# Value products on four column tiles, with sums that GpSimd adds first, in an attention and network kernel on one Trainium2 core

## The chip, the cores and the metric

The kernel runs on one NeuronCore of a Trainium2 chip. Its engines work side by side, each through its own queue: TensorE (products, into the PSUM banks), VectorE, ScalarE, GpSimd, and SyncE, which here only issues DMA transfers. They wait for each other by semaphores. The metric is the device time of one execution in microseconds (us), the median of several runs.

## What is computed

One block of a transformer on x of shape 4 x 1024 x 512, float32. The lines that matter:

```python
h = _layernorm(x) * (1 + ca) + sa
q = (h @ q_w.T + q_b).reshape(b, s, 16, 32)        # 16 heads of 32
k = h @ k_w.T + k_b                                # one key head, one value head for all
v = h @ v_w.T + v_b
scores = einsum('bqhd,bkd->bhqk', q, k) / 32 ** 0.5, causal, softmax over k
x = x + ga * (einsum('bhqk,bkd->bqhd', attn, v) @ o_w.T + o_b)
h = _layernorm(x) * (1 + cb) + sb
u = fwht(h * SU_ug) / 64                           # Walsh-Hadamard transform over 512
y = silu(u @ W_gate.T * sg) * (u @ W_up.T * su)    # 2048 wide
x = x + gb * (fwht(y * SU_dp) / 64) @ W_down.T * (Wscale_dp * 64)
```

## The kernel before

There are 64 heads in the attention stage (`ALL`, 4 batches of 16) and then 128 steps of the network stage (8 blocks of 512 rows by 16 tiles of the 2048). In the attention stage, every head's scores are kept transposed: keys on the 128 partitions, queries along the row. Only the causal part is computed. It is cut into nine units of up to 512 columns (`UNITS`: key tile, first query, width, column). For each unit TensorE computes scores into one of three score banks (L1468), ScalarE takes their exponent into `probs` (L772), and GpSimd clears the triangle above the diagonal of each 128 x 128 diagonal block (L847), 8 a head.

The softmax needs a maximum for each query beforehand. So beside the score of each unit TensorE computes one slot of scores the other way round (`SLOTS`, L1321), for the head that comes two later (`AHEAD`), into one of three side banks that are used in turn. VectorE reduces each slot to maxima (`reduce_slot`, L868 with the causal mask added and the masked scores written to an SBUF tile that nobody reads, L871 without a mask). After slot 8 `negate_maxima` (L880, L881) negates them. TensorE turns them into rows (`max_top`, L1328, in the next head, at `TOP_UNIT` = 1, also into a side bank), ScalarE copies these out (L634), and SyncE moves them into the rows of the queries' stack that add -max to the scores.

All side work uses these three banks in an order written out by hand (`side_work`): queries of four heads (2 x 12 products at the start of each fourth head, split by ScalarE and VectorE), layer norm rows of the next batch (`ROWS`), its keys and values in the head with n = 13 (`KV_STEP`; VectorE stacks the keys in `stack_keys` before the maximum slot of the same unit), output tiles of the last batch (`OUT_TILES`, two a head in heads 5 to 8 of a batch, 13 products each), and folding. Folding applies the second Hadamard transform to the rows of W_down, once: a first half ("across", 16 tiles, L1348) whose result is split into a rounded half by ScalarE and a rest by VectorE and stored to DRAM with both halves, and a second half ("along", 16 tiles, L1353), loaded from there, two fp32r products a tile. Both use rings of two buffers.

Value products (`weigh`, L1491): the weights are 64 columns, 32 of values and 32 of ones (`v_ones`), so that the same product gives the output and the sum of the exponents. The 64 columns go to one of two column tiles of TensorE, partitions 0 to 63 or 64 to 127 of a PSUM bank, and both tiles work side by side. `WEIGHED` gives the order: (tile, unit, key tile, first query, width, column). The products of a head stand in two parts. Part 0 (7 products, 1280 columns a tile) stands behind unit 8 and part 1 (5 products, 1024 columns a tile) behind unit 4 of the next head; these places are `PART_ENDS`. ScalarE empties a bank after each part (`evacuate`, L753). Two partial outputs and two partial sums are gathered by SyncE with four transfers a head (`gather`); VectorE adds and scales them once for four heads.

The engines' queues are in order. In a head, ScalarE's order for a unit is: exponent, what is in `ends`, the emptying of a part, then what is in `units`, where the negated maxima's copy is. VectorE's is: the unit's side work, then `ends`, then `prepare` (gains' floor, output weights and bias in head 7, `PROJECTION_STEP`), group work, and layer norm statistics (`STATS`). The square root of the layer norm's variance runs on ScalarE in head 6 of a batch (`ROOT_STEP`), which loads a table for it and then one for the exponent.

## Time and profile before

| | |
|---|---|
| median of 3 runs | 2063.32 us (2062.88 to 2069.54) |
| profiled execution | 2061.69 us |
| its span, first to last instruction | 2059.9 us |
| granted TensorE clock, mean | 0.988 of 2.4 GHz |
| TensorE busy | 1983.1 us (96%), 9120 matmuls |
| VectorE busy | 1196.9 us (58%) |
| ScalarE busy | 791.3 us (38%) |
| GpSimd busy | 149.3 us (7%) |

The span is cut by stage with the table of busy time by stretch. One head of the attention stage is then followed instruction by instruction on TensorE and VectorE. "Busy" of an engine is the union of its instructions, and TensorE's matmuls overlap, so their starts say more than their lengths. An instruction's start is in us from the span's start. PEclk is the granted TensorE clock, where 1.00 is 2.4 GHz.

### The profile page before, as it was taken

The numbers are of one execution on the slowest core, as the hardware profiler recorded it, in microseconds if no ns is written. First come the engines' busy times: TensorE is split into PE (matmuls) and PEld (weight loads), VectorE is DVE, ScalarE is ACT, GpSimd is POOL, SyncE is SP. The second block draws the span as 40 slices with busy tenths as digits, with TensorE's granted clock in tenths as the row PEclk, the third lists the DMA queues.
The fourth block names the chain that finished last, engine by engine and source line by source line (L and its number), as shares of the span: only waits on it lengthen the run. The fifth ranks groups of instructions, "written<-read, shape, count | busy, mean of one in ns | idle before, by whom it ended". The sixth has DMA issues, their size and how long they took to land.

```text
span 2059.9 us, 26392 instructions
## 1 busy us (share of the span) xinstructions
PE 1983.1 (96%) x9120; PEld 1469.9 (71%) x9120; DVE 1196.9 (58%) x2619; ACT 791.3 (38%) x1334; POOL 149.3 (7%) x522
## 2 busy tenths in 40 slices
PE   6999999999999999888999999999999999999998
PEld 3555666666666556545888888888888888888887
DVE  6678677676767665655555454445554454545434
ACT  3456555555556554455222222222212222222121
POOL 0111121111111111111000000000000000000000
PEclk9999999999999999989999999999999999999999
DMA  7443243333433476743534435334353343443431
GB/s 230 114 109 74 76 128 104 102 89 100 110 106 80 144 227 180 231 166 122 202 133 158 144 128 173 123 123 164 123 173 123 130 167 123 139 148 124 158 127 62
DMA packets 113659, 279.82 MB, mean 136 GB/s; under 512 B 27754, under 2 KB 33130, under 8 KB 113400
## 3 DMA queue, kind: packets, MB, share of 16 engines
q1 hardware_dynamic: 104168, 248.71, 39.0%
q10 hardware_dynamic: 9360, 29.43, 4.1%
q8 instruction: 74, 1.21, 0.2%
q14 instruction: 57, 0.47, 0.1%
HBM read 199.15 MB, written 35.93 MB: 114 GB/s over the span
## 4 chain that ended last, share of the span: by engine, by line
PE 53%; DVE 1%; DMA 1%; ACT 0%; issue 0%; SPq 0%; POOLq 0%; POOL 0%; DVEq 0%; ACTq 0%
PE banks L1266 34%; PE banks L1423 16%; PE banks L1491 1%; PE banks L1365 1%; PE banks L1359 1%; DMA upgate_raw<-in_w_ug 0%; PE banks L1468 0%; PE banks L1321 0%; DMA inverse_sums_dram<-sums 0%; DVE out_sb L1042 0%; DVE out_sb L1033 0%; DMA o_group<-o_raw 0%; PE banks L1334 0%; ACT h_crossed_split L691 0%; ACT probs L772 0%
## 5 line engine op out<-in xcount | busy, mean ns | idle before, releaser
L1266 PE MATMUL banks<-h_t_split,w_ring 128*128 128x512 f32 x3072 | 717.3, 389 | 0.8 <-DVE w_ring L1007 0.8
L1266 PEld LDWEIGHTS banks<-h_t_split,w_ring 128*128 128x128 f32 x3072 | 576.5, 188 | 121.0 <-DVE w_ring L1007 1.2
L708 ACT ACTIVATE silu_gate<-banks,scale_upgate 128x512 f32<-128x512 f32 x128 | 88.3, 690 | 800.6 <-PE banks L1266 800.6
L1423 PE MATMUL banks<-d_ring,y_split 128*128 128x512 f32 x1536 | 370.6, 390 | 0.1
L1015 DVE SCALAR_TENSOR_TENSOR y<-banks,scale_upgate,silu_gate 128x512 f32<-128x512 f32 x128 | 95.9, 749 | 433.4 <-ACT silu_gate L708 433.4
L772 ACT ACTIVATE probs<-banks 128x512 f32<-128x512 f32 x576 | 312.3, 597 | 84.6 <-PE banks L1468 79.3
L1423 PEld LDWEIGHTS banks<-d_ring,y_split 128*128 128x128 f32 x1536 | 287.2, 188 | 59.6 <-DVE y_split L1021 0.5
L1491 PE MATMUL banks<-probs,v_ones 128*64 128x512 f32 (+3 forms) x1536 | 292.4, 518 | 1.4 <-POOL probs L847 1.4
L1321 PE MATMUL banks<-k_stack,q_stacks 96*128 96x512 f32 (+3 forms) x768 | 245.7, 363 | 22.2 <-DVE q_split L889 11.2
L1468 PE MATMUL banks<-q_stacks,k_stack 98*128 98x512 f32 (+3 forms) x768 | 250.3, 368 | 4.9 <-ACT probs L772 4.9
L1491 PEld LDWEIGHTS banks<-probs,v_ones 128*64 128x64 f32 x1536 | 123.1, 142 | 161.7 <-issue 138.1
L847 POOL TENSOR_SCALAR_AFFINE_SELECT probs<-probs 128x128 f32<-128x128 f32 x512 | 147.0, 305 | 806.7 <-ACT probs L772 804.1
L1321 PEld LDWEIGHTS banks<-k_stack,q_stacks 96*128 96x128 f32 x768 | 140.1, 191 | 62.4 <-DVE max_all L868 16.7
L1468 PEld LDWEIGHTS banks<-q_stacks,k_stack 98*128 98x128 f32 x768 | 140.7, 191 | 57.7 <-issue 33.1
L871 DVE TENSOR_REDUCE max_all<-banks 128x1 f32<-128x512 f32 x256 | 165.0, 684 | 4.7 <-PE banks L1321 3.9
L1007 DVE TENSOR_TENSOR w_ring<-upgate_raw,w_ring 128x1024 fp32r<-128x1024 f32 x128 | 156.0, 1219 | 17.9 <-ACT w_ring L700 17.6
L868 DVE CUSTOM_DVE_ANT_0 masked_scores<-banks,mask_row,max_all 128x512 f32<-128x512 f32 (+3 forms) x256 | 132.0, 547 | 58.2 <-PE banks L1321 57.4
L753 ACT ACTIVATE o_raw<-banks 128x512 f32<-128x512 f32 x128 | 76.5, 597 | 206.9 <-PE banks L1491 206.9
L868 DVE CUSTOM_DVE_ANT_0 masked_scores<-banks,mask_row 128x512 f32<-128x512 f32 (+3 forms) x256 | 119.9, 486 | 48.0 <-PE banks L1321 46.7
L700 ACT ACTIVATE w_ring<-upgate_raw 128x1024 fp32r<-128x1024 f32 x128 | 135.1, 1056 | 9.4 <-DMA upgate_raw<-in_w_ug 9.4
L1266 PE MATMUL banks<-h_t_split,qw_group 128*128 128x512 f32 x384 | 92.1, 395 | 5.4 <-DVE h_t_split L898 3.0
L1266 PE MATMUL banks<-ow_split,o_split 128*128 128x512 f32 x384 | 94.4, 394 | 2.2 <-DVE max_all L868 2.1
(122 smaller groups left out, 1249.3 us busy)
## 6 DMA issues: line engine op xcount, KB each, us to landing
upgate_raw<-in_w_ug SPq DMA_DIRECT2D x128, 512.0 KB, 4.2
d_ring<-down_split_dram SPq DMA_DIRECT2D x128, 512.0 KB, 3.3
q_stacks<-q_split SPq DMA_DIRECT2D x192, 128.0 KB, 2.6
o_group<-o_raw SPq DMA_DIRECT2D x128, 128.0 KB, 2.3
x<-in_x SPq DMA_DIRECT2D x32, 256.0 KB, 4.3
o_group<-inverse_sums_dram SPq DMA_DIRECT2D x64, 128.0 KB, 2.7
x_and_residual<-in_x SPq DMA_DIRECT2D x32, 256.0 KB, 4.4
x_dram<-x_and_residual SPq DMA_DIRECT2D x32, 256.0 KB, 2.5
```

The costliest lines, as they stand in the source:

```text
L700: nc.scalar.activation(wr[g % 2][:, 0], ugr[g % UG_RING][:], ACT.Copy).then_inc(ug_cast, 1)
L772: nc.scalar.activation(pr[:, u, :], score_bank[:, at % SLOTS_SCORE, :], ACT.Exp, scale=SCALE).then_inc(exped, 1)
L847: last = nc.gpsimd.affine_select(out=triangle, in_=triangle, compare_op=ALU.is_ge, fill=0.0, base=0, pattern=[[1, P]], channel_multiplier=-1)
L868: last = nc.vector.tensor_tensor_reduce(out=masked_scores[:, i % 2, col:col + w], in0=part, in1=mask[:, HALF - w:HALF], scale=1.0, scalar= ...
L871: last = nc.vector.tensor_reduce(out, part, AX.X, ALU.max)
L1007: nc.vector.tensor_tensor(wr[g % 2][:, 1], ugr[g % UG_RING][:], wr[g % 2][:, 0].bitcast(F32), ALU.subtract).then_inc(ug_ready, 1)
L1015: nc.vector.scalar_tensor_tensor(out=y[:], in0=up_bank[:, s, :], scalar=sug[:, 0, f:f + 1], in1=sg[:, s, :], op0=ALU.mult, op1=ALU.mult).t ...
L1266: ins = nc.tensor.matmul(out, weights(a, k), moving(m, k), start=(k == 0 and a + m == 0), stop=(last and k == kts - 1 and a == 1))
L1321: last = nc.tensor.matmul(side[:, r, col:col + w], qst[0:96, s, qt * P:(qt + 1) * P], kst[0:96, b % 2, k0:k0 + w], start=True, stop=True)
L1423: last = nc.tensor.matmul(acc[:, t, :], ys[s][:, a, t * P:(t + 1) * P], dr[g % D_RING][:, m, :], start=(f == 0 and a + m == 0), stop=(f == ...
L1468: last = nc.tensor.matmul(score_bank[:, at % SLOTS_SCORE, col:col + w], kst[0:98, b % 2, kt * P:(kt + 1) * P], qst[0:98, s, q0:q0 + w], st ...
L1491: last = nc.tensor.matmul(obank[half * 2 * HD:(half + 1) * 2 * HD, c, q0 - c * HALF:q0 - c * HALF + w], vs[:, b % 2, kt, :], pr[:, u, col: ...
```

## The change

- Value products use four column tiles of 32 columns. Tiles 0 and 1 hold values, tiles 2 and 3 ones (in part 1 tile 2 holds values for queries from 256 on in its half, too). Parts are now halves of the queries: part 0 the first 512 (8 products, 640 columns a tile), part 1 the second (17 products, 1280 columns a tile). Each bank is written in one part only.
- The exponents of units 3 to 6 are added by GpSimd into `probs_added` (three additions a head), and ones are multiplied with that sum once. Part 1 waits for it. Unit 2 is needed by both parts and gets a second buffer for every other head.
- The parts stand behind units 2 (part 1 of the head before) and 6 (part 0). The turn of the negated maxima is at unit 2. Statistics, rows, output tiles, keys and folding move to other units and heads.
- Gathering takes six transfers a head; the group sum gets one more addition. The masked scores are written back into their bank.
- Folding's first half is stored in plain float32, without VectorE; the second half is one plain float32 product. Its rings have four buffers.
- The square root runs at the start of head 5 with the exponent's table loaded right behind it. Output weights are split at the start of heads 1 and 5, the bias at the start of head 1. Keys are stacked at the ends of units 2 and 6.

The diff, cut to its core:

```diff
-PART_ENDS, PARTS_OF_HEAD = (4, 8), 2
+PART_ENDS, PARTS_OF_HEAD, SHARED = (2, 6), 2, 2
+ADDED = (3, 4, 5, 6)
 WEIGHED = [
-    [(0, 0, 0, 0, 512, 0), (1, 4, 1, 512, 512, 0), (0, 3, 0, 512, 512, 0), (1, 1, 1, 128, 384, 0), (1, 1, 3, 384, 128, 384),
-     (0, 2, 6, 768, 256, 256), (1, 2, 2, 256, 256, 0)],
-    [(0, 5, 2, 512, 512, 0), (1, 6, 3, 512, 512, 0), (0, 7, 4, 512, 512, 0), (1, 8, 5, 640, 384, 0), (1, 8, 7, 896, 128, 384)],
+    [(0, "v", 0, 0, 0, 512, 0), (2, "s", 0, 0, 0, 512, 0), (1, "v", 1, 1, 0, 384, 128), (3, "s", 1, 1, 0, 384, 128),
+     (1, "v", 2, 2, 0, 256, 256), (3, "s", 2, 2, 0, 256, 256), (0, "v", 1, 3, 384, 128, 384), (2, "s", 1, 3, 384, 128, 384)],
+    [(0, "v", 3, 0, 0, 512, 0), (1, "v", 5, 2, 0, 512, 0), (2, "v", 7, 4, 256, 256, 256), (3, "s", 7, 4, 0, 256, 0),
+     (2, "s", 7, 4, 256, 256, 0), (3, "s", 2, 6, 256, 256, 256), (0, "v", 4, 1, 0, 512, 0), (1, "v", 6, 3, 0, 512, 0),
+     (2, "v", 8, 5, 128, 256, 256), (3, "s", 8, 5, 0, 128, 128), (3, "s", 8, 7, 384, 128, 384), (3, "s", None, None, 0, 512, 0),
+     (2, "s", 8, 5, 128, 256, 0), (0, "v", 7, 4, 0, 256, 0), (1, "v", 8, 5, 0, 128, 128), (2, "v", 2, 6, 256, 256, 256),
+     (1, "v", 8, 7, 384, 128, 384)],
 ]
-ROOT_STEP = 6
-OUT_TILES = {5: {2: 0, 6: 1}, 6: {2: 2, 6: 3}, 7: {2: 4, 6: 5}, 8: {2: 6, 6: 7}}
-ROWS = {(9, 4): (0, 0), (9, 8): (0, 1), (10, 4): (0, 2), (10, 8): (0, 3), (11, 2): (1, 0), (11, 4): (1, 1), (11, 8): (1, 2), (12, 4): (1, 3)}
+ROOT_STEP = 5
+OUT_TILES = {5: {4: 0, 8: 1}, 6: {4: 2, 8: 3}, 7: {4: 4, 8: 5}, 8: {4: 6, 8: 7}}
+ROWS = {(9, 2): (0, 0), (9, 6): (0, 1), (10, 2): (0, 2), (10, 6): (0, 3), (11, 2): (1, 0), (11, 4): (1, 1), (11, 6): (1, 2), (12, 2): (1, 3)}
-TOP_UNIT, FIRST_WEIGHED = 1, 6
+TOP_UNIT = 2
+STACK_UNITS = (2, 6)
-PROJECTION_STEP = 7
+PROJECTION_STEPS = (1, 5)
-            units[2].insert(0, ("kv", b + 1, 0))
-            units[5].insert(0, ("kv", b + 1, 1))
+            units[0].insert(0, ("kv", b + 1, 0))
+            units[4].insert(0, ("kv", b + 1, 1))
...
             def step(H):
                 begin, units, ends = side_work(H, ALL)
+                if n == ROOT_STEP and b + 1 < B:
+                    layer_norm_deviations(nc, act, T, eps, b + 1)
+                    nc.scalar.activation(scratch[:], eps[:], ACT.Exp)
...
+            def add_unit(H, i):
+                pool.wait_ge(exped, H * NU + ADDED[i] + 1)
+                if i == 1:
+                    pool.wait_ge(pv_done, H * PARTS_OF_HEAD)
+                else:
+                    pool.wait_ge(added, H * (len(ADDED) - 1) + i - 1)
+                first = pr[:, ADDED[0], :] if i == 1 else sb[:]
+                nc.gpsimd.tensor_tensor(sb[:], first, pr[:, ADDED[i], :], ALU.add).then_inc(added, 1)
+
             for H in range(ALL):
+                for u in range(NU):
+                    if u in TRIANGLES:
+                        clear_triangles(H, u)
+                    if u in ADDED[1:]:
+                        add_unit(H, ADDED.index(u))
...
-                        last = nc.vector.tensor_tensor_reduce(out=masked_scores[:, i % 2, col:col + w], in0=part, in1=mask[:, HALF - w:HALF],
+                        last = nc.vector.tensor_tensor_reduce(out=part, in0=part, in1=mask[:, HALF - w:HALF],
                                                               scale=1.0, scalar=out if k0 else -BIG, op0=ALU.add, op1=ALU.max, accum_out=out)
...
             def fold_tile(key):
-                    for a in range(2):
-                        last = nc.tensor.matmul(side[:, r, :], had[:], again[:, i % 2, a, :], start=a == 0, stop=a == 1)
+                    last = nc.tensor.matmul(side[:, r, :], had[:].bitcast(F32), again[:, i % FOLD_RING, :], start=True, stop=True)
...
             def weigh(H, part):
                 if part == 0:
-                    pe.wait_ge(masked, H * len(TRIANGLES) + 3)
-                    pe.wait_ge(exped, H * NU + PART_ENDS[0] + 1)
+                    pe.wait_ge(masked, H * len(TRIANGLES) + len([u for u in TRIANGLES if u <= SHARED]))
                 else:
                     pe.wait_ge(masked, (H + 1) * len(TRIANGLES))
+                    pe.wait_ge(added, (H + 1) * (len(ADDED) - 1))
+                products = WEIGHED[part]
+                for i, (tile, what, u, kt, col, w, to) in enumerate(products):
+                    weights = vs[:, b % 2, kt, :] if what == "v" else ones32[:]
+                    moving = sb[:, col:col + w] if u is None else pr[:, held(H, u), col:col + w]
+                    last = nc.tensor.matmul(obank[tile * HD:(tile + 1) * HD, part, to:to + w], weights, moving,
```

## Rows read from the trace of the kernel before

**Rows 1.** Busy time of TensorE over the span, from the page.
```profile
PE 1983.1 (96%) x9120; PEld 1469.9 (71%) x9120; DVE 1196.9 (58%) x2619; ACT 791.3 (38%) x1334; POOL 149.3 (7%) x522
```

**Rows 2.** Stretches with busy time (instructions) by engine, PEclk, DMA share, GB/s.
```profile
57.70:958.80 901.10, 848.17 (x4094) 545.01 (x4092) 622.21 (x1775) 493.41 (x941) 146.98 (x512) 0.97 0.44 123
958.80:2059.90 1101.10, 1094.38 (x4882) 906.38 (x4880) 539.39 (x764) 279.69 (x366) 0.00 (x0) 1.00 0.42 142
```

**Rows 3.** Timeline of TensorE, head 35: start, length, instruction, idle before.
```profile
518.51 0.50 PE L1468 MATMUL banks<-q_stacks,k_stack 98*128 98x512 f32 x1
518.85 0.40 PE L1321 MATMUL banks<-k_stack,q_stacks 96*128 96x512 f32 x1
...
520.04 0.50 PE L1321 MATMUL banks<-k_stack,q_stacks 96*128 96x512 f32 x1
...
521.42 1.94 PE L1491 MATMUL banks<-probs,v_ones 128*64 128x512 f32 x10
523.30 0.50 PE L1468 MATMUL banks<-q_stacks,k_stack 98*128 98x512 f32 x1
...
525.52 2.37 PE L1491 MATMUL banks<-probs,v_ones 128*64 128x512 f32 x14
527.83 0.50 PE L1468 MATMUL banks<-q_stacks,k_stack 98*128 98x512 f32 x1
```

**Rows 4.** Timeline of VectorE in the same head.
```profile
519.29 0.69 DVE L868 CUSTOM_DVE_ANT_0 masked_scores<-banks,mask_row 128x512 f32<-128x512 f32 x1 [0.95 <-PE banks L1321]
...
519.90 0.69 DVE L871 TENSOR_REDUCE max_all<-banks 128x1 f32<-128x512 f32 x1
...
525.50 0.55 DVE L868 CUSTOM_DVE_ANT_0 masked_scores<-banks,mask_row 128x384 f32<-128x384 f32 x1
...
527.00 0.08 DVE L868 DVE_READ_ACCUMULATOR2_ANT max_all<- 128x1 f32 x1
...
527.49 0.17 DVE L881 SCALAR_TENSOR_TENSOR neg_max<-max_all,neg_max 128x8 fp32r<-128x8 f32 x1
```

**Rows 5.** The value products as a group, from the page.
```profile
L1491 PE MATMUL banks<-probs,v_ones 128*64 128x512 f32 (+3 forms) x1536 | 292.4, 518 | 1.4 <-POOL probs L847 1.4
```

**Rows 6.** Timeline of VectorE behind an output tile, head 22.
```profile
349.50 0.69 DVE L941 TENSOR_TENSOR x_and_residual<-banks,gain_row 128x512 f32<-128x512 f32 x1 [2.73 <-PE banks L1334]
```

**Rows 7.** Groups of GpSimd by line and form: busy us, mean ns.
```profile
L847 POOL TENSOR_SCALAR_AFFINE_SELECT probs<-probs 128x128 f32<-128x128 f32 x512 | 147.0, 305 | 806.7 <-ACT probs L772 804.1
L833 POOL MEMSET mask_row<- 128x512 f32 x1 | 0.5, 528 | 0.0
```

**Rows 8.** Timeline of SyncE's queue: issues of DMA transfers in head 35.
```profile
525.31 1.22 SPq L414 DMA_DIRECT2D o_group<-o_raw  x2
```

**Rows 9.** Timeline of TensorE, waits in heads 6, 13, 38, 58.
```profile
143.01 0.50 PE L1321 MATMUL banks<-k_stack,q_stacks 96*128 96x512 f32 x1 [1.88 <-ACT neg_max_rows L634]
244.70 0.50 PE L1321 MATMUL banks<-k_stack,q_stacks 96*128 96x256 f32 x2 [1.18 <-DVE max_all L868]
561.57 0.73 PE L1266 MATMUL banks<-ow_split,o_split 128*128 128x512 f32 x2 [1.04 <-DVE max_all L868]
877.05 0.73 PE L1353 MATMUL banks<-fold_again,hadamard 128*128 128x512 f32 x2 [3.08 <-DMA fold_again<-down_across_dram]
```

**Rows 10.** Stretches as in rows 2: heads 8, 13, 58, 62.
```profile
161.80:181.40 19.60, 16.81 (x75) 11.02 (x74) 14.44 (x42) 10.37 (x19) 2.19 (x8) 0.91 0.22 53
230.20:250.10 19.90, 17.64 (x82) 11.49 (x81) 9.73 (x28) 7.29 (x14) 2.19 (x8) 0.91 0.47 129
870.40:891.50 21.10, 16.23 (x57) 8.31 (x55) 11.33 (x33) 8.09 (x15) 2.20 (x8) 0.76 0.92 318
931.70:946.90 15.20, 10.68 (x42) 5.36 (x40) 9.64 (x10) 8.47 (x17) 6.33 (x8) 0.78 0.27 70
```

**Rows 11.** Groups of TensorE: the folding's two products.
```profile
L1348 PE MATMUL banks<-fold_raw,across 128*128 128x512 f32 x32 | 17.4, 626 | 2.5 <-DVE fold_split L959 1.8
L1353 PE MATMUL banks<-fold_again,hadamard 128*128 128x512 f32 x32 | 12.6, 480 | 15.5 <-DVE max_all L868 4.4 <-DMA fold_again<-down_across_dram 3.1 <-ACT neg_max_rows L634 2.9
```

More of the change, by code:

```diff
@@ L360, in side_drained, with held @@
         engine.wait_ge(side_free[r], len([place for place in places.values() if place % SLOTS_SIDE == r]))
+    def held(H, u):
+        return NU if u == SHARED and H % 2 else u
     def free_bank(g, k):
@@ L671, in fold_transfers @@
                             store_fold((kind, i))
-                        if i < 2 and (ALL - left) * NU == H * NU + u + LOAD_BEFORE:
-                            load_fold(kind, i)
+                        if i == 0 and (ALL - left) * NU == H * NU + u + LOAD_BEFORE:
+                            for first in range(FOLD_RING):
+                                load_fold(kind, first)
             def turn(nb, k, bank):
@@ L918, in add_halves @@
                 if half:
+                    chain.link(last)
+                    last = nc.vector.tensor_tensor(on[:, S - REST:S], on[:, S - REST:S], og_rest[:], ALU.add)
                     last.then_inc(group_taken, 1)
```

188 lines of the change are left out of this document (101 added, 87 removed), and 4 rows, old and new, of the table UNITS.

## Prediction

> **What bounds the kernel now.** The page comes first: TensorE is busy 96% of the span, so the question for each edit is what it does to TensorE's order of work [rows 1]. The table by stage shows three stretches: 57.7 us of start, 901.1 us of attention (64 heads), 1101.1 us of network [rows 2]. The change touches the attention stage and its folding; the network's instructions stay as they are. In attention TensorE is busy 848 of 901 us, VectorE 622, ScalarE 493 and GpSimd 147 [rows 2].
>
> The timeline of one plain head (33 or so look like it) runs from score matmul to score matmul, 518.51 to 527.83, 9.32 us [rows 3]. Its value products stand in two lumps: part 1 of the head before from 521.42 to 523.30 (1.88 us) and part 0 from 525.52 to 527.83 (2.31 us), 4.19 us in all. Between lumps a score and a maximum product alternate every 0.235 us or so; the first after a lump takes 0.34 us. Only one of them is held up: the maximum product of unit 2, at 520.04, and by a tenth. It needs the side bank that VectorE's first reduction of the head frees, and that reduction ends at 519.98 [rows 3, 4]. So VectorE already stands right behind TensorE, and the 2.31 us lump is where it catches up: it works on the last two slots from 525.50 to 527.00 and has the negated maxima at 527.66, 0.17 us before the lump ends and three products before they are wanted [rows 3, 4].
>
> **Value products.** A float32 product is two passes (1536 records for 64 x 12 products [rows 5]), each at two cycles a column: part 1 holds 1024 columns for each of two tiles, 1024 x 4 / 2.4 GHz = 1.71 us, and takes 1.88; part 0 holds 1280, 2.13 us, and takes 2.31. So 0.17 to 0.18 us a lump is overhead and the rest columns, on both tiles at once. After the change part 0 has 640 columns a tile on four tiles (1.07 us) and part 1 has 1280 (2.13 us). With the same overhead: 1.24 + 2.30 = 3.54 us, 0.65 less than 4.19, 41 us over 64 heads, if nothing else binds. That four tiles run side by side is in no row; two do. Bounds: all of it (-41 us), or only two at a time, 7680 columns x 4 / 2.4 / 2 = 6.4 us a head instead of 3.2 (+205 us). I take full overlap, since the two tiles keep the full rate each and the order cycles through the tiles.
>
> The Trainium skill (TensorE: Matmul & The Clock Gate, "Measured speedup vs the span model") gives 2.38 times for three column tiles, not 3. By that the four would take 3.2 x 3 / 2.38 = 4.0 us a head, and the change would be worth 53 us less than my sum. No row here shows more than two tiles.
>
> **Where the lumps stand.** Part 1 moves from behind unit 4 to behind unit 2, part 0 from behind unit 8 to behind unit 6, and the product of the negated maxima from unit 1 to unit 2. Now slots 7 and 8 are issued after part 0, and nothing long stands between them and that product. Count from the start of maximum product 7: 0.44 us until VectorE starts (518.85 to 519.29), slots 7 and 8 1.50 (525.50 to 527.00), negation 0.66 (to 527.66) [rows 3, 4]: the negated maxima are there at 2.60. TensorE gets to them after about 2.0 us (eight products of 0.23 to 0.29). Then maximum product 2 needs the bank of slot 0, which VectorE starts only after the negation: + 0.03 + 0.70 + 0.05 = 3.38 us, where TensorE would be at 2.1. So 1.3 us of wait, in two pieces. A second one: ScalarE empties part 1 (0.50 us to its next instruction) before it copies the negated maxima out of their bank (0.25 us), so maximum product 4 starts 0.92 us behind score 3 and not 0.81, and pays 0.1 for weights that aren't preloaded.
>
> The new head from maximum product 7 to the next: 3.38; to part 1, 0.34 + 0.09 = 0.43; part 1 2.30; score 3 to part 0, 0.92 + 0.34 + 3 x 0.24 + 0.32 = 2.30; part 0 1.24; score 7 and on, 0.34. Sum 9.99 us against 9.32: +0.67 us, although the products are 0.65 us shorter.
>
> By kind of head (62 have the product of the negated maxima):
> - 35 plain or nearly so: 35 x 0.67 = +23.5.
> - 15 that begin with queries (5.6 us of products hide the wait): 15 x (0.21 - 0.65) = -6.6.
> - 9 behind an output tile at unit 8. VectorE has to do gain and residual (0.69, and as long again) between slots 7 and 8 [rows 6], and TensorE has only 1.75 us of other products: 4.0 - 1.75 = 2.25 us of wait, 1.6 a head, +14.5.
> - 3 behind transposed values: +0.
> - Some 23 heads have layer norm rows or folding at unit 6 now, and the VectorE and ScalarE work behind it delays slot 7 by 0.4 to 0.5: +10.
> - The last part 1 is 0.43 longer.
>
> Together **+42 us**. VectorE's masked maxima now write to PSUM; no row has such an output. The reduction without a wide output takes as long as the masked one [rows 4], so the output costs nothing now; I take nothing and, for the range, 0.06 us each way on the five in the chain: 47 heads x 0.3 = 14 us.
>
> **GpSimd.** It clears 512 triangles at 0.305 us and is idle otherwise [rows 7]. It now adds three times 512 columns a head. No row has a two-input operation on it; the memset of 512 takes 0.53, and four times a 128-wide select is 1.2. I take 1.2. Part 1 now waits for the sums, and behind that wait stands all of TensorE. From score 3: exponent 4 ends at 1.85, then 3a + 3 x 0.25 + 0.1, and part 1 starts at 9.99 - 2.30 = 7.7: it doesn't bind below a = 1.65 us.
>
> The Trainium skill (GPSIMD Engine Reference, "3.1 Elementwise — side-by-side cycle accounting") gives 4497 ns for an add of 2048 columns, 1.12 us for 512 if it scales; the sum stays the same. No run here shows it yet.
>
> SyncE gathers with six transfers a head and not four, 1.2 us more of issue at 0.6 each [rows 8]: it has 3 + 1 + 6 = 10 in 10 us, 6.3 us, not on the path. VectorE gets one more 256-wide sum in 15 heads, under queries.
>
> **Repairs.** I price each by a head's excess over its kind.
> - Square root: two table loads and the root hold ScalarE in head 6, and TensorE waits 1.88 [rows 9]. Before the queries they are covered. Head 6 takes 13.9 instead of 9.8 us, heads 22 and 38 lose 1.04 each [rows 9]: -6.
> - Output weights and bias: VectorE's work on them pushes the negated maxima of head 8 back; it takes 19.6 us, TensorE busy 16.8, where its kind takes 14.9 [rows 10]: -4.5.
> - Keys: a wait of 1.18 and a clock of 0.91 in head 13, and the same in 29 and 45 [rows 9, 10], 3.6 us each. Keys at units 0 and 4 with the stacking behind the lumps leave some: -8.5.
> - Folding: first half without VectorE and half the bytes, a ring of four. Head 49 -1.8; heads 54 to 57 lose some 2 each and get new waits of the kind above, -3; head 58 takes 21.1 us where 12 would do, with a wait of 3.08 for a load and a clock of 0.76, and head 59 is like it [rows 9, 10]: 16 us of excess, of which the stores and the block's load keep a third, -11; head 62, with the crossing, takes 15.2 us, TensorE busy 10.7 [rows 10], -4. Against that the second half's product in plain float32 is two passes of 0.43, not two of 0.2: the first half's takes 17.4 us for 16 tiles, the second's 12.6 [rows 11], with 0.4 a tile in columns, +6.4. Net -13.4.
>
> Together **-32 us** (-20 to -50).
>
> **Clock.** It falls in heads where TensorE waited 1.5 us or more in a short while (1.18 and 0.34 more; 1.88; 3.08) and stays at 1.00 in those with one wait of up to 1.04 [rows 9, 10]. The new 1.3 us lie between; those behind output tiles lie above. A stretch at 1.2 GHz of the kind seen costs about 1.7 us. I take five new ones less what VectorE catches up meanwhile: +5, between 0 and 60.
>
> **Sum.** The profiled execution took 2061.69 us with a span of 2059.9; +42 - 32 + 5 gives 2076.7. The median of the runs, 2063.32, is 1.6 above the profiled one: **2078 us**.
>
> **Rivals.** A measurement can tell 0.3%, 6 us, from no change.
> - The forecast: 2078, its own range 2060 to 2095, 0.50.
> - A, faster: the wait for the negated maxima is smaller and the repairs give all of their excess. It decides at a wait of some 0.6 us a head. For it: the removed waits are in the rows; against it: the VectorE chain is five rows long and TensorE's part of it three. With half of the wait (-31) and repairs of -45: 2035; with no wait at all (62 x 1.5) 1990. 0.25.
> - B, the clock: half of the 47 waits bring a stretch at 1.2 GHz, 24 x 1.7 = 40 less the 5: 2113. 0.12.
> - C, GpSimd binds: an add over 1.65 us, or VectorE held up by it. At 2.0 us, 3 x 0.35 x 47 = 49: 2127. For it: its only rows are of one input. 0.07.
> - D, the four tiles don't run together: at best +53, 2131, at worst 2283. The change then doesn't do what it says. 0.06.
>
> Most of A and 0.02 of the forecast are faster by over 0.3%; 0.11 of the forecast and 0.02 of A lie within; the rest is slower. Range: 2030 (leaves the better half of A) to 2118 (leaves D and the longer half of C).
>
> **What will show it.** Right: a plain head of 9.9 to 10.1 us; lumps of 2.3 and 1.24 us; TensorE waiting 0.5 to 0.8 us for the negated maxima and again for slot 0's bank; heads 6, 8 and 58 to 62 shorter. Wrong: plain heads of 8.7 us (no wait); part 1 waiting on GpSimd; lumps over 4 us; masked maxima of another length than 0.69; granted clock under 0.95 over attention.

## Result, and the profile after

The changed kernel takes 2190.55 us (median of 4 runs, 2183.77 to 2193.87), the kernel before beside it 2065.49 us (2062.88 to 2069.54): a ratio of 1.060, 95% interval 1.057 to 1.063. The forecast was 2078 us with a range of 2030 to 2118. So the direction was right, and the size was off by more than 100 us, 73 us beyond the end of the range. The profiled execution took 2189.16 us with a span of 2187.4, mean granted clock 0.964 (0.988 before).

The page's busy times of the changed kernel, which answer to [rows 1]:

```profile
PE 2030.1 (93%) x10784; PEld 1510.0 (69%) x10784; DVE 1236.8 (57%) x2621; ACT 791.5 (36%) x1337; POOL 400.0 (18%) x714
```

The stretches of attention and network, which answer to [rows 2] (the stretch, its length, busy time and instructions of TensorE, its weight loads, VectorE, ScalarE, GpSimd, granted clock, DMA share, GB/s):

```profile
60.90:1074.80 1013.90, 881.16 (x5757) 582.60 (x5756) 661.05 (x1775) 493.59 (x944) 398.04 (x704) 0.93 0.38 103
1074.80:2187.40 1112.60, 1105.56 (x4880) 906.73 (x4880) 539.99 (x765) 279.76 (x366) 0.00 (x0) 1.00 0.43 140
```

Of the 127.5 us of longer span 112.8 are in attention (901.1 to 1013.9), 11.5 in the network (1101.1 to 1112.6), where I had taken nothing, and 3.2 in the start, which tells nothing of the change: in the other runs below the start takes 57.9 to 62.1 us, 59.0 and 61.4 in two runs of one kernel. In attention TensorE's idle time goes from 52.9 us (901.1 - 848.2) to 132.7, and its clock from 0.97 to 0.93: 7% of 1013.9 less 3% of 901.1 is 44 us of work that the lower level costs. GpSimd goes from 147 to 398 us.

The waits of TensorE that are new, over the whole span (what waits, for what: us in total, times, longest):

```profile
PE banks L1379 <- DVE max_all L919: 49.9, 77, 1.2
PE banks L1386 <- DVE neg_max L932: 39.0, 41, 4.5
PE banks L1379 <- ACT neg_max_rows L664: 13.0, 27, 0.5
PE banks L1386 <- DVE q_split L940: 12.7, 9, 1.7
```

The first two are the waits of the forecast, for slot 0's bank (L1379 is the maximum products) and for the negated maxima (L1386 is their transpose). The third is for ScalarE's copy of the negated maxima out of their bank, 0.48 us each time where the forecast had a delay of 0.1. The fourth wasn't foreseen: where queries stand ahead of a head, the transpose waits 1.1 to 1.7 us for VectorE's split of the queries, behind which the sums of the head group now stand, too (before, one maximum product waited 0.75 us for that split). A plain head of the changed kernel, as head 35 in [rows 3, 4]. TensorE and then VectorE in head 31, 524.64 to 534.96:

```profile
523.83 0.40 PE L1379 MATMUL banks<-k_stack,q_stacks 96*128 96x384 f32 x2
...
525.63 0.41 PE L1525 MATMUL banks<-q_stacks,k_stack 98*128 98x256 f32 x2
526.59 0.28 PE L1386 MATMUL banks<-ident,neg_max 128*16 128x128 f32 x1 [0.56 <-DVE neg_max L932]
527.49 0.50 PE L1379 MATMUL banks<-k_stack,q_stacks 96*128 96x512 f32 x1 [0.62 <-DVE max_all L919]
527.93 0.62 PE L1547 MATMUL banks<-probs,values 128*32 128x512 f32 x3
...
530.22 0.50 PE L1525 MATMUL banks<-q_stacks,k_stack 98*128 98x512 f32 x1
...
531.21 0.50 PE L1379 MATMUL banks<-k_stack,q_stacks 96*128 96x512 f32 x1
...
532.60 0.62 PE L1547 MATMUL banks<-probs,values 128*32 128x512 f32 x1
...
533.81 0.50 PE L1525 MATMUL banks<-q_stacks,k_stack 98*128 98x512 f32 x1
```

```profile
524.27 0.57 DVE L919 CUSTOM_DVE_ANT_0 banks<-banks,mask_row 128x384 f32<-128x384 f32 x1 [0.39 <-PE banks L1379]
...
525.81 0.14 DVE L919 DVE_READ_ACCUMULATOR2_ANT max_all<- 128x1 f32 x1
...
526.37 0.17 DVE L932 SCALAR_TENSOR_TENSOR neg_max<-max_all,neg_max 128x8 fp32r<-128x8 f32 x1
526.68 0.70 DVE L919 CUSTOM_DVE_ANT_0 banks<-banks,mask_row 128x512 f32<-128x512 f32 x1
```

Part 1 lasts from 527.93 to 530.22, 2.29 us, part 0 from 532.60 to 533.81, 1.21 us, and the chain is that of the forecast: slot 7's product at 523.83, VectorE on slots 7 and 8 from 524.27 to 525.95, negated maxima at 526.54, the transpose at 526.59, slot 0 read until 527.44, its bank's next product at 527.49. So the plain head (10.31 us for a forecast 9.99) was forecast well; most of the loss is elsewhere. The next table has the lengths of heads (from the first score product of a head to that of the next) summed by kind, worked out from the traces of four kernels. "Repairs alone" and "parts at 1 and 8" are experiments below.

| Heads | before | changed | repairs alone | parts at 1 and 8 |
|---|---|---|---|---|
| 15 to 20, 31 to 36 (plain, or with queries) | 135.7 | 147.4 | 135.6 | 136.6 |
| 21 to 24, 37 to 40 (output tiles) | 138.6 | 152.3 | 138.5 | 142.9 |
| 9 to 12, 25 to 28, 41 to 44 (layer norm rows) | 146.5 | 200.8 | 146.5 | 154.9 |
| 46 to 57 (folding) | 189.7 | 220.6 | 194.6 | 192.1 |
| 58 to 63 | 88.5 | 96.4 | 75.3 | 84.6 |
| the other 14 | 202.2 | 196.4 | 187.0 | 185.3 |

The twelve heads with layer norm rows lose 54 us, those with folding 31. The stretches of two of the first kind, heads 10 and 11 (before: 10.62 and 11.33 us):

```profile
198.32:214.57 16.25, 13.30 (x85) 8.33 (x84) 10.47 (x27) 7.50 (x16) 6.32 (x12) 0.79 0.22 50
214.57:231.27 16.70, 12.89 (x89) 8.03 (x88) 11.81 (x29) 8.57 (x17) 7.51 (x13) 0.90 0.24 53
```

TensorE's waits at the start of head 10, which before the change had none there:

```profile
200.44 0.50 PE L1379 MATMUL banks<-k_stack,q_stacks 96*128 96x512 f32 x1 [1.24 <-DVE max_all L919]
...
201.80 0.38 PE L1386 MATMUL banks<-ident,neg_max 128*16 128x128 f32 x1 [0.63 <-DVE neg_max L932]
...
202.70 0.80 PE L1379 MATMUL banks<-k_stack,q_stacks 96*128 96x512 f32 x1 [0.52 <-DVE max_all L919]
```

A maximum product already waits 1.24 us for a bank before the two waits of the plain head come. Over the twelve heads with rows TensorE's idle time goes from 3.7 to 33.5 us, and its time at 1.2 GHz from none to 58.0 us. At the price of a stretch that experiment 2 gives, the latter is some 25 us, so idle time (30) and clock (25) make up the 54 in about equal parts.

### The profile page after: what moved, and what is told of

Its sections match the earlier page's. It is cut to its first block, busy times and chain, and to the rows that moved or that the text cites. A ratio compares the mean times of both kernels' runs of the same rounds, so it can differ in the third digit from the quotient of the medians.

```text
span 2187.4 us, 30242 instructions
## 1 busy us (share of the span) xinstructions
PE 2030.1 (93%) x10784; PEld 1510.0 (69%) x10784; DVE 1236.8 (57%) x2621; ACT 791.5 (36%) x1337; POOL 400.0 (18%) x714
## 4 chain that ended last, share of the span: by engine, by line
PE 74%; DVE 13%; issue 5%; ACT 1%; DMA 1%; SPq 0%; DVEq 0%; ACTq 0%; POOL 0%; POOLq 0%
PE banks L1324 37%; PE banks L1480 16%; PE banks L1547 10%; DVE banks L919 5%; PE banks L1379 4%; PE banks L1525 3%; DVE max_all L922 1%; DVE max_all L919 1%; PE banks L1406 1%; PE banks L1410 1%; DVE q_split L940 1%; DVE o_split L986 1%; DVE o_group L968 1%; PE banks L1422 1%; PE banks L1416 1%
## 5 line engine op out<-in xcount | busy, mean ns | idle before, releaser
L1324 PE MATMUL banks<-h_t_split,w_ring 128*128 128x512 f32 x3072 | 727.6, 392 | 1.1 <-DVE w_ring L1059 1.1
L1379 PE MATMUL banks<-k_stack,q_stacks 96*128 96x512 f32 (+3 forms) x768 | 255.9, 376 | 65.8 <-DVE max_all L919 49.9
L922 DVE TENSOR_REDUCE max_all<-banks 128x1 f32<-128x512 f32 x256 | 174.0, 689 | 189.2 <-PE banks L1379 185.8
L1547 PE MATMUL banks<-probs,values 128*32 128x512 f32 (+3 forms) x1792 | 277.2, 516 | 3.8 <-POOL probs L882 3.8
L1547 PE MATMUL banks<-probs,ones 128*32 128x256 f32 (+3 forms) x1280 | 244.4, 433 | 0.0
L1379 PEld LDWEIGHTS banks<-k_stack,q_stacks 96*128 96x128 f32 x768 | 140.7, 192 | 127.4 <-DVE max_all L919 64.6
L1547 PEld LDWEIGHTS banks<-probs,values 128*32 128x32 f32 x1792 | 116.4, 122 | 121.7 <-issue 74.4
L893 POOL TENSOR_TENSOR probs_added<-probs_added,probs 128x512 f32<-128x512 f32 x128 | 167.6, 1309 | 48.9 <-ACT probs L810 33.1
L893 POOL TENSOR_TENSOR probs_added<-probs 128x512 f32<-128x512 f32 x64 | 81.9, 1280 | 390.3 <-ACT probs L810 390.3
L919 DVE CUSTOM_DVE_ANT_0 banks<-banks,mask_row 128x512 f32<-128x512 f32 (+3 forms) x256 | 131.0, 515 | 33.9 <-PE banks L1379 27.1
L919 DVE CUSTOM_DVE_ANT_0 banks<-banks,mask_row,max_all 128x512 f32<-128x512 f32 (+3 forms) x256 | 133.1, 555 | 11.2 <-PE banks L1379 3.4
```

The lines of the kernel that those rows point to most:

```text
L893: nc.gpsimd.tensor_tensor(sb[:], first, pr[:, ADDED[i], :], ALU.add).then_inc(added, 1)
L919: last = nc.vector.tensor_tensor_reduce(out=part, in0=part, in1=mask[:, HALF - w:HALF], scale=1.0, scalar=out if k0 else -BIG, op0=ALU.add ...
L922: last = nc.vector.tensor_reduce(out, part, AX.X, ALU.max)
L1324: ins = nc.tensor.matmul(out, weights(a, k), moving(m, k), start=(k == 0 and a + m == 0), stop=(last and k == kts - 1 and a == 1))
L1379: last = nc.tensor.matmul(side[:, r, col:col + w], qst[0:96, s, qt * P:(qt + 1) * P], kst[0:96, b % 2, k0:k0 + w], start=True, stop=True)
L1547: last = nc.tensor.matmul(obank[tile * HD:(tile + 1) * HD, part, to:to + w], weights, moving, start=tile not in [p[0] for p in products[:i ...
```

## Experiments

The experiments ran in three sessions beside the kernel before, which took 2061.6, 2060.6 and 2063.3 us (experiments 1 to 4; 5 to 7 and 9; 8 and 10 to 12); ratios are to it. The changed kernel's 1.060 is 2185 us there.

**1. Part 0 behind unit 8.**

```diff
-PART_ENDS, PARTS_OF_HEAD, SHARED = (2, 6), 2, 2
+PART_ENDS, PARTS_OF_HEAD, SHARED = (2, 8), 2, 2
```

> The changed kernel with one number changed: the value products of the first half of the queries (1.21 us in the changed kernel's trace) stand behind unit 8 of their head and not behind unit 6. My theory: the 127 us come from the two short waits of each head (0.56 us for the negated maxima and 0.62 us for slot 0's bank in head 31), from their larger forms in heads that carry rows or folds, and from the clock falls that such waits bring (98 us more at 1.2 GHz than before). With 1.2 us of products between unit 8 and the next head VectorE has that much more time, so both waits nearly go: a plain head of 9.2 to 9.5 us where it was 10.31, less time at 1.2 GHz, 2190 less 50 for the waits and less 20 to 40 for the clock: 2100 to 2120 us. The rival, that the placement matters little and the products on four tiles or GpSimd's sums cost the time: 2180 to 2195 us.

Measured: 2145.59 us, 1.041 (1.039 to 1.043), 40 us less than the changed kernel where I expected 65 to 85. In attention 967.1 us, clock 0.97. Head 31 takes 10.07 us and keeps one wait, at the same place:

```profile
516.51 0.28 PE L1386 MATMUL banks<-ident,neg_max 128*16 128x128 f32 x1
517.41 0.51 PE L1379 MATMUL banks<-k_stack,q_stacks 96*128 96x512 f32 x1 [0.62 <-DVE max_all L919]
```

The 1.2 us of products take the wait for the negated maxima away, not that for slot 0's bank; and the heads with rows stay long (194.4 us). The most comes back in the heads with folding (195.2 us for 220.6). The placement matters, but one lump isn't enough.

**2. No additions on GpSimd.** Its `add_unit` and TensorE's wait for it are left out; the last product with ones reads `pr[:, 8]`, so the sums are not those of the softmax.

> The changed kernel without GpSimd's three additions a head: the last product with ones reads one unit of exponentials in place of the added units, so the sums of the weights are not the reference's. My theory: the additions (1.28 us each, 3.9 us a head) end ahead of the products that read them, so 2185 to 2192 us, the network and the plain head (10.31 us) as they are. The rival, that GpSimd binds or that its additions slow VectorE beside them: the 64 heads lose their waits, 2100 to 2150 us.

Measured: 2168.84 us, 1.051 (1.049 to 1.054): 16 us less, between the two theories. Plain heads are as they were (10.33 us in head 31), so TensorE doesn't wait for the sums. But heads 10 and 11 go to 13.85 and 14.24 us, and the first wait of head 10, 1.24 us above, is gone:

```profile
195.75 0.28 PE L1384 MATMUL banks<-ident,neg_max 128*16 128x128 f32 x1 [0.60 <-DVE neg_max L930]
...
196.66 0.49 PE L1377 MATMUL banks<-k_stack,q_stacks 96*128 96x512 f32 x1 [0.62 <-DVE max_all L917]
```

What differs there is VectorE. In order: VectorE and GpSimd at the end of head 10 in the changed kernel, then VectorE at the same place without additions:

```profile
213.20 0.92 DVE L948 CAST h_t_split<-kv 128x512 fp32r<-128x512 f32 x1
214.15 1.68 DVE L949 TENSOR_TENSOR h_t_split<-kv,h_t_split 128x512 fp32r<-128x512 f32 x1
```

```profile
213.98 1.29 POOL L893 TENSOR_TENSOR probs_added<-probs_added,probs 128x512 f32<-128x512 f32 x1
```

```profile
206.68 0.69 DVE L947 TENSOR_TENSOR h_t_split<-kv,h_t_split 128x512 fp32r<-128x512 f32 x1
```

VectorE's subtraction from SBUF to SBUF takes 0.69 us alone and 1.68 when it begins beside an addition of GpSimd: it ends 0.56 us behind the addition's end. The groups say the same (attention; count, busy us, mean ns): the subtraction has a mean of 1057 ns in the changed kernel and 693 without additions, the rounding ahead of it 584 and 426, the keys' subtraction 1166 and 681.

```profile
L949 DVE TENSOR_TENSOR h_t_split<-kv,h_t_split 128x512 fp32r<-128x512 f32 x24 | 25.4, 1057 | 0.8
...
L956 DVE TENSOR_TENSOR k_stack<-kv,k_stack 32x512 fp32r<-32x512 f32 x6 | 7.0, 1166 | 0.2
```

```profile
L947 DVE TENSOR_TENSOR h_t_split<-kv,h_t_split 128x512 fp32r<-128x512 f32 x24 | 16.6, 693 | 0.8
```

The reductions, which read PSUM, take 689 ns in both. So the additions cost TensorE time through VectorE: 12.9 us over the twelve heads with rows, and heads 14 and 30, which begin behind the keys' stacking, go from 25.6 to 20.4 us. In all attention is 21.5 us shorter, although the eight heads with output tiles are 8.3 us longer: these have 27.3 us at 1.2 GHz for 6.8. The Trainium skill (SBUF — State Buffer, "SBUF: two separate sides") says that VectorE and GpSimd share a port pair, and that an operation with two SBUF inputs and one of GpSimd that reads SBUF exclude each other for the whole instruction. The 1.68 and 0.69 us above agree with that in the main: held back to the end of the addition, the subtraction would end 0.69 us behind it, and it ended 0.56 behind.

The two kernels also price the clock. Head 23 has the same waits in both (2.02 us), at full clock in the changed kernel and with a stretch of 3.41 us at 1.2 GHz without additions:

```profile
387.33:404.63 17.30, 15.26 (x103) 10.94 (x102) 9.63 (x27) 8.04 (x15) 6.27 (x11) 1.00 0.36 103
```

```profile
378.06:396.82 18.76, 16.71 (x103) 11.51 (x102) 9.63 (x27) 8.03 (x15) 2.34 (x8) 0.91 0.31 95
```

One such stretch costs 1.46 us. Attention has 146 us at 1.2 GHz in the changed kernel and 48 before. The 98 us more are as much as 29 stretches of this length (many stand two together), 42 us by this price, as by the mean clock above.

**3. Padding ahead of the network's tiles.**

```diff
-ones32=place(s, "ones", [P, HD]),
+ones32=place(s, "ones", [P, HD]), pad=place(s, "pad", [P, 3 * HD]),
```

(`under_h2` and `under_parts` grow by the same 96 columns.)

> The changed kernel with 96 unused columns (384 bytes of each partition) laid behind the 32 columns of ones, so that every tile behind them starts a multiple of 512 bytes from where the tiles ahead of them do, as in the kernel before. In the changed kernel each step of the network's odd blocks takes 0.17 us more than before, of the even blocks none; the odd blocks read the one transposed input that moved by 128 bytes. My theory: TensorE's stream of the moving operand costs about 7 ns more in each of 24 products where that operand starts at this address; with the pad the 64 steps lose 11 us: 2176 to 2182 us. The rival, that it is something else of the odd blocks (their loads, their position): 2187 to 2193 us.

Measured: 2182.79 us, 1.057 (1.053 to 1.061), in total no difference that the intervals can tell, and neither range is hit. The trace tells more. Block 1 (16 steps, odd) and block 2 (even) of the changed kernel, then block 1 with the pad of 96 columns, and block 1 with a pad of 32 columns (experiment 8):

```profile
1237.40:1374.10 136.70, 136.70 (x601) 111.29 (x600) 67.21 (x95) 35.78 (x47) 0.00 (x0) 1.00 0.43 139
1374.10:1508.50 134.40, 134.40 (x602) 111.28 (x600) 67.20 (x95) 35.77 (x47) 0.00 (x0) 1.00 0.44 141
```

```profile
1245.90:1380.10 134.20, 134.20 (x601) 111.27 (x600) 67.21 (x95) 35.77 (x47) 0.00 (x0) 1.00 0.42 141
```

```profile
1129.60:1263.80 134.20, 134.20 (x601) 111.26 (x600) 67.17 (x95) 35.78 (x47) 0.00 (x0) 1.00 0.43 141
```

The 2.5 us of each odd block, 0.16 us a step, go with the pad; from the start of the network's first down product to that of its last it is 1086.9 us for 1095.1. The total hides it: attention took 1020.1 us in this execution, with 20 us more at 1.2 GHz than in the changed kernel's.

**4. The repairs alone.** The kernel before with `PROJECTION_STEPS`, the keys at units 0 and 4 stacked at 2 and 6, the square root at a head's start, and the new folding at units 4 and 8; the crossing at the end of attention moves along.

> The kernel before with the repairs alone: the square root at a head's start with the exponential's table loaded behind it, the output weights in heads 1 and 5, the keys' product at units 0 and 4 and their stacks at units 2 and 6, and the folding with one product a tile, four buffers and a fourth head at the end; the value products, their placement and GpSimd's work as before. My forecast had 32 us for them: 2065 less 32 is 2033; what the changed trace shows of the heads that carry them (heads 6 and 8 3.5 us shorter each, 13, 29 and 45 4.6 shorter, 14, 30 and 46 3.4 longer, 3 to 5 some 8 longer in all, 58 and 59 10.5 shorter) makes it less, so 2035 to 2050 us. The rival, that the repairs bring their own clock falls and waits (the heads from 46 on are 31 us longer in the changed trace): 2060 to 2090 us.

Measured: 2041.24 us, 0.990 (0.988 to 0.992): 20 us less than before. Its stretches: attention, head 8, head 13, head 58, head 54:

```profile
59.00:936.60 877.60, 839.78 (x4094) 539.17 (x4092) 613.14 (x1759) 492.28 (x944) 149.05 (x512) 0.99 0.42 117
```

```profile
163.28:178.64 15.36, 15.12 (x76) 10.47 (x74) 11.40 (x31) 10.10 (x19) 2.72 (x8) 1.00 0.27 68
227.48:243.69 16.21, 15.62 (x82) 10.71 (x80) 9.85 (x28) 7.27 (x14) 2.50 (x8) 1.00 0.38 106
861.35:874.20 12.85, 11.66 (x55) 6.44 (x53) 10.33 (x32) 7.29 (x14) 2.19 (x8) 1.00 0.97 319
781.10:800.65 19.55, 17.62 (x81) 11.32 (x79) 11.15 (x32) 7.46 (x14) 2.26 (x8) 1.00 0.71 208
```

Head 8 lost 4.3 us and the three heads of the keys 3.65 each. The folding gave 8.3 over heads 46 to 63: head 58 lost 8.3 and heads 59 and 62 7.2 together, but heads 54 to 56 are 0.8 longer each, 57 1.6, and 46 is 2.5 longer, with a new wait of 1.16 us for an exponent and 3.41 us at 1.2 GHz. The square root gave nothing, since in this kernel it stood in head 6, where no queries cover it; in the changed kernel it stands in head 5, and head 6 is 3.6 us shorter.

**5. Both lumps around the head's boundary.**

```diff
-PART_ENDS, PARTS_OF_HEAD, SHARED = (2, 6), 2, 2
+PART_ENDS, PARTS_OF_HEAD, SHARED = (1, 8), 2, 2
```

(and units 2 and 6 become 1 and 8 in `STATS`, `ROWS` and `FOLDS`, with 1, 3, 5, 8 where there are four.)

> The changed kernel with the value products of the second half behind unit 1 and of the first half behind unit 8, and with the statistics, the row transposes and the folding tiles moved from units 2 and 6 to units 1 and 8. With the first half alone behind unit 8 the kernel took 2146 us (4.1% over the kernel before); its head 31 kept one wait, 0.62 us for the bank of slot 0, which VectorE reads behind the negated maxima. My theory, that these waits come from how little of TensorE's other work stands between the maxima of one head and slot 2 of the next: with both lumps (1.24 and 2.29 us) in that place the wait goes, a plain head is 9.2 to 9.4 us (10.31 in the changed kernel, 9.32 before), the time at 1.2 GHz falls to some 30 us, and the kernel to 2080 to 2105 us. The rival, that the second half's products then wait for the exponentials and masks of unit 8: a wait of 0.5 to 1.5 us at the first value product of each head, 2130 to 2200 us.

Measured: 2072.15 us, 1.006 (1.004 to 1.008). This is 113 us less than the changed kernel and under my range, too: nearly the whole loss is the placement. Attention:

```profile
60.70:957.10 896.40, 822.70 (x5758) 562.55 (x5756) 650.32 (x1775) 490.52 (x944) 407.11 (x704) 0.97 0.42 117
```

TensorE's idle time is 73.7 us of it (132.7 in the changed kernel), and the time at 1.2 GHz 48 us (146): by the price above, 59 us of waits and 42 of clock are 101 of the 117 us that attention lost. Head 31 takes 9.67 us, 0.3 more than my range, with a wait as in the rival's mechanism:

```profile
475.04 0.44 PE L1379 MATMUL banks<-k_stack,q_stacks 96*128 96x512 f32 x1
476.18 0.62 PE L1547 MATMUL banks<-probs,values 128*32 128x512 f32 x3 [0.69 <-POOL probs L882]
```

```profile
472.69 2.70 POOL L893 TENSOR_TENSOR probs_added<-probs_added,probs 128x512 f32<-128x512 f32 x2
475.35 1.52 POOL L882 TENSOR_SCALAR_AFFINE_SELECT probs<-probs 128x128 f32<-128x128 f32 x6
```

Here GpSimd does bind: the masks of units 7 and 8 stand behind its additions, which end at 475.35.

**6. Masked scores to SBUF again.** `out=part` becomes a tile of bytes in SBUF.

> The changed kernel with the masked scores of the maxima written to an SBUF tile of bytes again and not back to their PSUM bank (four small tiles are put together to make room, so that every address moves by 32 or 64 bytes). In the changed trace each of the 504 accumulator reads behind those operations takes 0.141 us, 0.082 before. My theory, that VectorE's chain of the last slots, the negated maxima and slot 0 sets the two waits of a head: six such reads stand on it (slots 6 to 8), so each head is 0.3 to 0.4 us shorter, 20 to 25 us in all, and some of the clock falls go with it: 2145 to 2165 us where the changed kernel's is 2185 beside a before of 2062. The rival, that the chain has slack there and the reads cost nothing: 2180 to 2190 us.

Measured: 2183.99 us, 1.061 (1.058 to 1.063), no difference, as the rival had it. The reads are as short as before (0.082 us), but head 31 takes 10.25 us where it took 10.31, and not 0.3 to 0.4 less. The timeline of the changed kernel has the reason: a read begins together with the next operation of VectorE.

```profile
522.95 0.14 DVE L919 DVE_READ_ACCUMULATOR2_ANT max_all<- 128x1 f32 x1
522.95 0.62 DVE L919 CUSTOM_DVE_ANT_0 banks<-banks,mask_row,max_all 128x384 f32<-128x384 f32 x1
```

Only a read for which somebody waits is on the path, 0.14 us in place of 0.08, once or twice a head. My theory held in one kind of head: heads 18, 19, 34 and 35, with layer norm statistics behind units 2 and 6, take 10.25 us where they took 10.54 to 10.57. Over attention that is 6 us, too few to be told in the total.

**7. The transpose of the maxima at unit 1** (`TOP_UNIT = 1`).

> The changed kernel with the transpose of the negated maxima behind unit 1 of the next head, as in the kernel before, and not behind unit 2. My theory of the VectorE chain: the transpose waits 0.5 us longer there, but the bank of slot 0 is then asked for one slot later in the ring's order, and what is lost at one is saved at the other, so a plain head is 9.9 to 10.4 us and the kernel 2155 to 2190 us: the placement of the transpose alone is no remedy. The rival, that the transpose at unit 2 is itself what costs the heads their 1.2 us: a plain head of 9.3 us, 2110 to 2130 us.

Measured: 2154.31 us, 1.046 (1.044 to 1.049): 31 us less, just under the lower end I gave my own theory, and far from the rival's. The waits show what it does: one place in the place of two.

```profile
PE banks L1386 <- DVE neg_max L932: 81.1, 46, 4.5
...
PE banks L1379 <- DVE max_all L919: 10.4, 23, 1.2
```

A head like 35 is 0.35 us shorter (10.21), heads 6 and 7 are 0.1 shorter, and heads 15 and 31 are 1.0 and 1.1 longer, with 3.41 us at 1.2 GHz that they didn't have; the most comes from the heads with rows (187.6 us for 200.8) and folding (46 to 57: 204.5 for 220.6). TensorE's idle time is 127 us, the clock no better, so the transpose's place was one cost of its own, not the cause.

**8. The lumps alone, tables left at 2 and 6,** with a pad of 32 columns.

> The changed kernel with the value products alone behind units 1 and 8; statistics, row transposes and folding tiles stay behind units 2 and 6. And 32 unused columns behind the ones, so that the tiles behind them start 256 bytes off from those ahead (modulo 512), where the changed kernel has 128 and the padded one none. With everything moved the kernel took 2072 us. My theory, that the two lumps behind the maxima carry the gain and the tables little: 2075 to 2100 us. The rival, that what cost the changed kernel its 120 us was VectorE's and ScalarE's side work at units 2 and 6: 2110 to 2150 us. In the network: if only a whole multiple of 512 bytes frees the odd blocks, their steps stay at 8.33 us; if 256 bytes are enough, they are 8.16 us.

Measured: 2071.07 us, 1.004 (1.002 to 1.005), 4 us under my range. Attention is 904.7 us, 8 more than with the tables moved, which are back in the heads with rows (169.9 us for 154.9), while those with folding are shorter (187.3 for 192.1); the network is free of its 11 us, as the stretch shown under 3 has it. So the lumps carry 109 of the 117 us of attention. With an offset of 256 bytes the odd blocks are as fast as with none.

**9. Both edits, 5 and 6.**

> The two edits together: value products behind units 1 and 8 with the tables moved along, and the masked scores written to SBUF. If the first edit takes the waits of plain heads away, the second adds only what it saves in heads with rows, folds and output tiles: 5 to 15 us less than the first edit alone, 2070 to 2095 us. If the first leaves the waits, the second takes 20 to 25 us of them.

Measured: 2067.14 us, 1.003 (1.002 to 1.004), 3 us under my range and 5 us less than with the first alone: 0.1 to 0.2 us in many heads (head 47 11.15 for 11.25, head 14 9.85 for 10.04) and one stretch at 1.2 GHz less, in head 46.

**10. The last addition behind the masks.**

```diff
-                    if u in ADDED[1:]:
+                    if u in ADDED[1:-1]:
                         add_unit(H, ADDED.index(u))
+                add_unit(H, len(ADDED) - 1)
```

(on top of 5; TensorE waits for `added` only at the product that reads the sums.)

> The kernel with value products and tables at units 1 and 8 (2072 us), and GpSimd's last addition behind its masks of units 7 and 8, with the wait for it at the product that reads it. In that kernel's head 31 GpSimd's additions end at 475.35 us, its masks at 476.2, and the first value product waits 0.69 us for them, while the exponentials ended at 473.2. My theory, that GpSimd binds this placement by these 0.7 us in some 35 heads: the wait goes, a plain head is 8.95 to 9.05 us where it was 9.67, and the kernel 2072 less 20 to 28: 2044 to 2052 us. The rival, that another wait takes its place (the last addition, or the bank of slot 0 as in the kernel with one lump moved): 2060 to 2072 us.

Measured: 2062.00 us, 0.9995 (0.998 to 1.001), 14 us less than 5 by the ratios where I expected 20 to 28, in the rival's range. Plain heads are what I expected, here head 31:

```profile
468.17:477.07 8.90, 8.83 (x79) 6.15 (x75) 7.44 (x23) 5.74 (x12) 5.82 (x12) 1.00 0.64 170
```

8.90 us without a wait is 0.42 less than before [rows 3]: that is what four tiles are worth where nothing waits. Over heads 15 to 20 and 31 to 36 it is 129.5 us for 135.7. Other heads don't gain: those behind output tiles (143.8 for 142.9), and heads 2 to 4 (42.9 for 40.8, with 3.4 more us at 1.2 GHz).

**11. On top of 10, the pad of 96 columns, and the network's first products ahead of the last value products.**

> That kernel with the 96 unused columns of the padded one and with the network's first up and gate products ahead of the last head's second value products, which wait 3.5 us for masks there. The pad took 9 us from the network's 64 odd steps, the last head is 9 us longer than before and has 3.5 us of that wait: 2048 less 9 less 3 to 5 is 2032 to 2040 us. The rival, that clock falls eat the gains: 2045 to 2060 us.

Measured: 2056.32 us, 0.997 (0.995 to 0.998). The pad gave its 8 us in the network (1087.3 from the first to the last down product, 1095.3 in experiment 10). The last edit gave nothing: the wait for masks became one of 2.9 us for the network's first weights. The rival's range, not mine.

**12. The repairs alone, beside it.**

> The kernel before with the repairs alone once more, beside the kernel above on one chip: 2036 to 2045 us. If the kernel above is the faster, the four tiles and GpSimd's sums gain something once they are placed well; my sum for them without any wait was 41 us less, of which the added waits and the clock leave 0 to 10.

Measured: 2043.98 us, 0.991 (0.989 to 0.992). The repaired kernel before is 12 us faster than the best placement of the four tiles that I tried, and it is the fastest of all: the answer to the question in my expectation is no.

## Why the prediction was wrong

The step that failed is the size of the placement term, +42 us. Its mechanism, that VectorE's last slots stand without a lump to cover them, is the right one, and moving the lumps took the loss away. But it was priced in the plain head, and the heads with layer norm rows and folding, where it is many times as large and brings the clock down, got +10 us. The clock term (+5) failed with it. The terms one by one:

- **Value products**: right. 1.21 and 2.29 us for forecast 1.24 and 2.30: 1280 columns a tile take as long on four tiles as they took on two (2.31). The 2.38 times of the Trainium skill (TensorE: Matmul & The Clock Gate, "Measured speedup vs the span model") would have given 4.0 us by the prediction's estimate, for 3.50 measured; it is a figure for three tiles, and for these streams the measurement decides against it. Rival D is out.
- **Placement, plain heads**: the mechanism was right, each of the two waits (0.56 and 0.62 us) was within the 0.5 to 0.8 that I named, and the head was 10.31 us for 9.99. The missing 0.3 stand in VectorE's chain: from maximum product 7 (523.83) to maximum product 2 (527.49) it is 3.66 us for 3.38. Slots 7 and 8 with the negation take 0.11 longer, VectorE starts on slot 0 0.14 us behind the negation for 0.03, and is done with it after 0.76 for 0.70. Where layer norm statistics stand at units 2 and 6, the head is 10.55. Behind an output tile (heads 22 to 24, 38 to 40) six heads are 11.5 us longer in all, forecast 1.6 each, and head 23 waits 2.02 us for 2.25: near.
- **Placement, heads behind queries**: the sign was wrong. I let the queries hide the wait and had 15 heads 0.44 us shorter each; heads 17 and 33 are 0.43 and 0.45 longer, with a wait of 1.13 us for the queries' split on VectorE and 0.30 for slot 0's bank, for 0.75 in one wait before. If all 15 are like these, an estimate, it is 13 us.
- **Placement, heads with rows or folding**: this term was mis-sized. I gave 23 heads 0.4 to 0.5 us each, +10 us. The twelve with rows alone cost 54 us (4.5 each), the twelve with folding 26 against the repaired kernel (220.6 for 194.6). Three things come together there: VectorE's and ScalarE's work behind unit 6 now stands directly ahead of slots 7 and 8, with no lump to cover it; GpSimd's additions at the same units stretch it, one subtraction from 0.69 to 1.68 us; and the clock falls there (0.79 in head 10, 0.90 in head 11). I had priced the first. Without additions 12.9 us of the 54 go, with the lumps moved 31 (experiment 8), with lumps and tables 46 (experiment 5).
- **GpSimd**: 1.2 us was 1.28 to 1.31, and in the changed kernel it doesn't bind in a plain head, as forecast. Its price through VectorE I named in half a sentence of rival C and gave nothing: 16 us in all (experiment 2).
- **Clock**: the sum had +5 and the range up to 60; it was 42 to 44, of which some 25 lie in the heads with rows and are in their 54, too. The price of a stretch, 1.7 us, was near (1.46). The number of stretches was wrong (five for 29).
- **Repairs**: 32 us forecast, 20 measured alone. Weights right (4.3 for 4.5), keys better (11.0 for 8.5), folding worse (8.3 for 13.4), the square root nothing for 6 alone, 3.6 in head 6 of the changed kernel.
- **Network**: "the network's instructions stay as they are" was true and wasn't enough; a tile that they read moved by 128 bytes, +11 us.
- **The last head**: I added 0.43 us for the last part 1. It waits 3.78 us for GpSimd's masks, and the head has 12.8 us at 1.2 GHz; it is 22.2 us for 11.9, and in the other placements up to experiment 10 it still takes 19.7 to 22.3.
- **Rival A's lower end**: a slip. Without any wait (62 x 1.5 = 93 us) and with 13 us more of repairs 2078 would be 1972 and not 1990. Nothing else rests on it.

In sum, the 127.5 us are -23.5 for the repairs in attention (901.1 to 877.6), +136.3 for value products, placement and clock (877.6 to 1013.9) where I had 47 (42 + 5), +11.5 in the network, where I had nothing, and +3.2 in the start, within what it varies by. The rival that came nearest in its mechanism is B, the clock, and a part of C; neither had the size. What stays open: a part of the 29 stretches also appears in kernels with the same waits and in other heads (head 23 above), so the traces price the clock but don't tell for one head whether it will fall. No run took the clock's part away from that of the waits, so the two halves of the 54 us are worked out and not measured apart.

## What to carry to other kernels

A block of work that doesn't wait is cover for the engine that runs behind: before shortening or moving it, count for every kind of loop turn, the rare ones most, what it covers; here moving two lumps by one and two units was worth 109 us of attention, more than twice what the shorter products could save. Work given to an idle GpSimd was paid here by VectorE where both worked in SBUF, while VectorE's reductions from PSUM kept their length; whether additions placed beside these alone would be free wasn't tried. When a tile's size changes, look where the tiles behind it start, and at stages that the change doesn't touch.

## What the runs showed of the hardware

- A moving operand of TensorE (the 512 columns that stream through the weights) that started 128 bytes off, modulo 512, from where the network's other tiles did cost 2.5 us in 16 steps of 24 float32r products of 512 columns: 0.16 us a step, between 6 and 7 ns a product. In the changed kernel the network's tiles start at 160 modulo 512 bytes and the odd blocks' input at 288 (slow); it starts at 160 with 96 columns of pad and at 416 with 32 (both fast). In experiment 6 the same pair is 128 and 256, and the odd blocks are slow again. Whether the weights' or another tile's address is the other half of the pair wasn't tried.
- Four column tiles of 32 columns ran float32 products at the rate of two tiles of 64: 1280 columns a tile in 2.29 us, 2.31 before.
- A float32 addition of 512 columns on GpSimd takes 1.28 to 1.31 us. VectorE's subtraction of 512 columns from SBUF to SBUF took 0.69 us alone and 1.68 beside one (experiment 2).
- The accumulator read behind a masked maximum takes 0.141 us when the operation's wide output goes to PSUM and 0.082 when it goes to SBUF, and it begins together with the next operation of VectorE.
